# Scan stage of a hybrid block on one core: the drives of two states by TensorE from diagonal matrices, one state left to GpSimd, ScalarE's five placed anew

## What is computed

```python
def selective_scan(u, dt, A, Bm, Cm, Dvec):
    dA  = exp(dt[..., None] * A)                        # decay of state n
    dBu = dt[..., None] * Bm[:, :, None, :] * u[..., None]   # drive of state n
    def step(h, xs):
        dA_t, dBu_t, C_t = xs
        h = dA_t * h + dBu_t
        return h, einsum('bdn,bn->bd', h, C_t)
    ys = scan(step, 0, over the tokens)
    return ys + u * Dvec
```

## Time and profile before

| | |
|---|---|
| median of 3 runs | 2160.12 us (2157.04 to 2160.7) |
| profiled execution, its own time | 2158.89 us |
| its span, first to last instruction | 2157.1 us |
| scan stage | from about 780 to 1592 us of the span |
| busy over the span | PE 93%, PEld 71%, DVE 69%, ACT 56%, POOL 67% |
| mean granted TensorE clock | 0.977 |

### The profile page before, as it was taken

The page is one execution under the profiler, slowest core; times in us unless marked ns, Lnnn a source line. Parts: engine busy times, 40 slices in busy tenths (PEclk is TensorE's granted clock), DMA queues, the critical chain, the costliest instruction groups (busy, mean ns, idle before and its releaser), DMA issues. The chain is left out here.

```text
span 2157.1 us, 42455 instructions
## 1 busy us (share of the span) xinstructions
PE 2008.0 (93%) x14350; PEld 1535.7 (71%) x14351; DVE 1497.0 (69%) x2749; ACT 1201.5 (56%) x2399; POOL 1440.7 (67%) x972
## 2 busy tenths in 40 slices
PE   7998999999999988989988889898789999999998
PEld 5886448999999545656655556565554489999994
DVE  6887684333333579999999999999976833333335
ACT  5775423222222279999989888989844132222222
POOL 6774005777767249999999999989940067777670
PEclk9999999999999989999999999989899999999999
DMA  8000100000001422332322323222233000000014
GB/s 304 0 1 11 30 1 20 26 24 25 24 24 26 111 96 90 101 106 93 100 89 100 99 89 98 100 91 97 83 138 143 1 22 26 24 26 24 24 25 121
DMA packets 72198, 141.91 MB, mean 66 GB/s; under 512 B 9835, under 2 KB 43629, under 8 KB 69910
## 3 DMA queue, kind: packets, MB, share of 16 engines
q1 hardware_dynamic: 62998, 121.86, 16.9%
q0 software_dynamic: 9088, 18.63, 3.0%
HBM read 123.81 MB, written 16.65 MB: 65 GB/s over the span
## 5 line engine op out<-in xcount | busy, mean ns | idle before, releaser
L2269 POOL TENSOR_TENSOR m_seen<-m_state,experts 128x1024 f32<-128x1024 f32 x256 | 600.7, 2369 | 59.8 <-DVE m_state L2323 54.2
L2323 DVE TENSOR_TENSOR_SCAN m_state<-experts,ps 128x512 f32<-128x512 f32 x448 | 540.1, 1235 | 0.5 <-PE ps L1860 0.5
L1877 PE MATMUL ps<-ident,m_seen 128*128 128x128 f32 x2048 | 278.8, 281 | 36.9 <-POOL m_seen L2269 36.9
L1877 PEld LDWEIGHTS ps<-ident,m_seen 128*128 128x128 f32 x2048 | 243.2, 145 | 75.8 <-POOL m_seen L2269 54.9
L2082 ACT ACTIVATE experts<-delta,experts 128x512 f32<-128x512 f32 x448 | 291.3, 713 | 1.0 <-DVE delta L2349 0.5
L1591 POOL COPY f_weights<-experts 128x1898 f32 x142 | 252.3, 1777 | 23.8 <-issue 23.5
L1414 PE MATMUL first_up_ps<-f_xT,f_weights 128*128 128x128 f32 x1988 | 241.4, 275 | 1.7 <-issue 1.7
L1414 PE MATMUL ps<-zu,f_weights 128*128 128x128 f32 x1988 | 241.4, 275 | 1.7 <-issue 1.7
L1414 PEld LDWEIGHTS first_up_ps<-f_xT,f_weights 128*128 128x128 f32 x1988 | 233.2, 192 | 2.5 <-issue 2.5
L1414 PEld LDWEIGHTS ps<-zu,f_weights 128*128 128x128 f32 x1988 | 233.2, 192 | 2.5 <-issue 2.5
L2303 DVE TENSOR_TENSOR ps<-m_delta_u,ps 128x512 f32<-128x512 f32 x286 | 193.4, 676 | 15.4 <-PE ps L1835 15.1
(11 more groups left out here) (451 smaller groups left out, 3904.2 us busy)
## 6 DMA issues: line engine op xcount, KB each, us to landing
experts<-m_rows SPq DMA_DIRECT2D x144, 512.0 KB, 3.6
experts<-in_experts SPq DMA_DIRECT2D x17, 1461.0 KB, 18.6
tokens<-f_rows SPq DMA_DIRECT2D x8, 512.0 KB, 5.3
f_rows<-expert_out SPq DMA_DIRECT2D x8, 512.0 KB, 7.0
f_cols<-expert_out SPq DMA_DIRECT2D x8, 512.0 KB, 7.0
out<-X SPq DMA_DIRECT2D x4, 512.0 KB, 3.2
X<-in_x SPq DMA_DIRECT2D x4, 448.0 KB, 5.9
f_xin<-tokens,f_take POOLq DMA_INDIRECT x71
```

The source lines that it names most:

```text
L1877: mm = pe.matmul(Y[:, i // 2, at:at + P], seen[:, n % SEEN, h, i * P:(i + 1) * P], ident[:], is_transpose=True, start=(n == 0 and at == 0) ...
L2269: pool.tensor_tensor(seen[:, n % SEEN], state[:, n % RING], c_rep[:, Q % C_RING, n % C_GROUP, :].unsqueeze(1).to_broadcast([P, HALF, SEG]) ...
L2323: dve.tensor_tensor_scan(state[:, n % RING, h, :], decay_, drive_, before_, ALU.mult, ALU.add).then_inc(s_state, 1)
```

## The change

- AWAY is state 12 alone; GpSimd makes its drive after step 4 (before: state 4 after step 15 of the unit before, state 12 after step 6).
- DIAGONAL = (2, 11): the drive of these two comes from TensorE alone. `cross` multiplies, for each of the four pieces i of 128 tokens, the turned delta_u (tokens on the partitions, 128 by 128) with a diagonal matrix whose diagonal holds B's row for these tokens; the result is the drive, channels on the partitions, in PSUM. Four fp32 multiplications of 128 by 128 a half.
- The diagonal matrices (128 by 4 * 128 for each of the two states) are laid out by DMA: a DRAM array m_diagonal is written once with zeros from an SBUF tile that GpSimd has cleared (512 KB); in each unit SP scatters the 512 numbers of a row onto the diagonals (elements of 4 bytes, L1776 of the changed kernel) and loads the matrix (256 KB, L1785) ahead of the second and the third group of C.
- ACROSS = (4, 6, 8, 10, 14): ScalarE still scales for five states, but others, at steps 0, 3, 5, 6 and 10 (before: state 2 at step 15 of the unit before, 5 at 1, 8 at 3, 11 at 6, 14 at 9).
- VectorE multiplies the drives of 8 states (0, 1, 3, 5, 7, 9, 13, 15) for 9 (0, 1, 3, 6, 7, 9, 10, 13, 15).
- The decay of state 4 goes into the ring dA like the others, at step 1; those of 5 and 6 are made at steps 2 and 3.
- b_rep holds one row for two.

```diff
-                AWAY = (4, 12)
-                AWAY_AT = {15: 4, 6: 12}
-                ACROSS = (2, 5, 8, 11, 14)
-                ACROSS_AT = {15: 2, 1: 5, 3: 8, 6: 11, 9: 14}
+                AWAY, AWAY_AT = 12, 4
+                ACROSS = (4, 6, 8, 10, 14)
+                ACROSS_AT = {0: 4, 3: 6, 5: 8, 6: 10, 10: 14}
+                DIAGONAL = (2, 11)
+                WIDTH = len(DIAGONAL) * SEG
...
+                DIAGONAL_BEFORE = (1, 2)
...
+                diagonal = lodge(WIDTH).rearrange("p (k t) -> p k t", t=SEG)
+                diagonal_out = nc.dram_tensor("m_diagonal", (P * (WIDTH + 1),), F32, kind="Internal").ap()
+                whole_out = diagonal_out[0:P * WIDTH].rearrange("(p k t) -> p k t", k=len(DIAGONAL), t=SEG)
+                entries_out = diagonal_out.rearrange("(p f) -> p f", f=WIDTH + 1)[:, 0:WIDTH:P].rearrange("p (k i) -> p k i", i=SEG // P)
...
-                DECAYED = [[2, 3], [5], [6], [4], [], [7, 8], [9], [10], [11], [], [13], [12], [14], [15], [NS], [NS + 1]]
+                DECAYED = [[2, 3], [4], [5], [6], [], [7, 8], [9], [10], [11], [], [13], [12], [14], [15], [NS], [NS + 1]]
...
+                        sp.wait_ge(s_hT, 1)
+                        sp.dma_start(whole_out, diagonal).then_inc(s_rows_out, 16)
+                        sp.wait_ge(s_rows_out, 16)
...
-                            sp.wait_ge(s_rows_out, 16 * (V + 1))
-                            wait(sp, s_away, len(AWAY) * V)
-                            sp.dma_start(b_rep, rows_out[V % 2][AWAY[0]:NS:AWAY[1] - AWAY[0], :].unsqueeze(0).to_broadcast([P, len(AWAY), SEG])).then_inc(s_b_rep, 16)
+                            sp.wait_ge(s_rows_out, stored(V))
+                            for k, n in enumerate(DIAGONAL):
+                                wait(sp, s_diagonal[k], 16 * V)
+                                sp.dma_start(entries_out[:, k, :], rows_out[V % 2][n, :].rearrange("(i p) -> p i", p=P), allow_slow_non_contiguous=True).then_inc(s_rows_out, 16)
+                            wait(sp, s_away, V)
+                            sp.dma_start(b_rep, rows_out[V % 2][AWAY:AWAY + 1, :].to_broadcast([P, SEG])).then_inc(s_b_rep, 16)
                             for g in range(GROUPS):
+                                if g in DIAGONAL_BEFORE:
+                                    k = DIAGONAL_BEFORE.index(g)
+                                    sp.wait_ge(s_rows_out, stored(V) + 16 * len(DIAGONAL))
+                                    if V:
+                                        sp.wait_ge(s_upright, (nth_upright[(V - 1) * NS + DIAGONAL[k]] + 1) * HALF)
+                                    sp.dma_start(diagonal[:, k, :], whole_out[:, k, :]).then_inc(s_diagonal[k], 16)
...
+                        def cross(G, h):
+                            U, n = divmod(G, NS)
+                            k = DIAGONAL.index(n)
+                            pe.wait_ge(s_diagonal[k], 16 * (U + 1))
+                            pe.wait_ge(s_read0, nth0["du", U] + 1)
+                            pe.wait_ge(s_read1, nth1["du", U] + 1)
+                            wait(pe, s_state, (G - B_RING) * HALF + h + 1)
+                            for i in range(TILES):
+                                mm = pe.matmul(PB[n % B_RING][:, h, i * P:(i + 1) * P], across[:, i, h * P:(h + 1) * P], diagonal[:, k, i * P:(i + 1) * P], start=True, stop=True)
+                            mm.then_inc(s_upright, 1)
...
                         def refill(G, h):
+                            if G % NS in DIAGONAL:
+                                cross(G, h)
...
-                        scale(ACROSS[0])
...
-                            if n + 1 == AWAY[0]:
-                                decays(G + 1)
...
+                        pool.memset(diagonal, 0.0)
                         pool.memset(hT[:, :, 0:PAD], 0.0).then_inc(s_hT, 1)
...
-                        drive(AWAY[0])
                         for G in range(STEPS):
...
-                            if n in AWAY_AT:
-                                m = AWAY_AT[n] + (NS if AWAY_AT[n] < n else 0)
-                                if U * NS + m < STEPS:
-                                    drive(U * NS + m)
+                            if n == AWAY_AT:
+                                drive(U * NS + AWAY)
```

More of the change, by code:

```diff
@@ L1658, in mamba @@
                 scaled = lodge(SCALED * TILES * DI).rearrange("p (r i d) -> p r i d", r=SCALED, d=DI)
+                diagonal = lodge(WIDTH).rearrange("p (k t) -> p k t", t=SEG)
+                assert room[0] <= LODGERS * EXPERT
+                diagonal_out = nc.dram_tensor("m_diagonal", (P * (WIDTH + 1),), F32, kind="Internal").ap()
+                whole_out = diagonal_out[0:P * WIDTH].rearrange("(p k t) -> p k t", k=len(DIAGONAL), t=SEG)
+                entries_out = diagonal_out.rearrange("(p f) -> p f", f=WIDTH + 1)[:, 0:WIDTH:P].rearrange("p (k i) -> p k i", i=SEG // P)
                 rows_out = [nc.dram_tensor(f"m_rows_{k}", (2 * NS, SEG), F32, kind="Internal").ap() for k in range(2)]
@@ L1682, in mamba @@
                 s_turned, s_back, s_y = ts("turned"), ts("back"), ts("y")
+                s_diagonal = [ts(f"diagonal{k}") for k in range(len(DIAGONAL))]
                 s_scaled, s_upright, s_hT = ts("scaled"), ts("upright"), ts("hT")
@@ L1699, in tokens, with stored @@
                     return (t // C * STREAMS + s) * TPB + t % C * TILES
+                def stored(V):
+                    return 16 * (2 + V * (1 + len(DIAGONAL)))
                 def columns_in(U, k):
@@ L1732, in mamba @@
                 decayed = [0, 1] + [U * NS + m for U in range(N_UNITS) for n in range(NS) for m in DECAYED[n] if U * NS + m < STEPS]
-                assert all(n + 1 not in AWAY or DECAYED[n][-1] == n + 1 for n in range(NS))
+                assert DECAYED[AWAY - 1][-1] == AWAY
                 nth_decay = {G: k for k, G in enumerate(decayed)}
-                driven = [G for G in range(STEPS) if G % NS not in AWAY + ACROSS]
+                driven = [G for G in range(STEPS) if G % NS != AWAY and G % NS not in ACROSS + DIAGONAL]
+                nth_upright = {G: k for k, G in enumerate(G for G in range(STEPS) if G % NS in ACROSS + DIAGONAL)}
+                turned_over = [G for G in range(STEPS) if G % NS in ACROSS]
                 nth_across = {G: k for k, G in enumerate(G for G in range(STEPS) if G % NS in ACROSS)}
                 nth_drive = {G: k for k, G in enumerate(driven)}
-                nth_away = {G: k for k, G in enumerate(G for G in range(STEPS) if G % NS in AWAY)}
                 kept = [(U, n) for U in range(N_UNITS) if UNITS[U][2] % C < C - 1 for n in range(0, NS, 2)]
@@ L2041, in round_high @@
                             act.wait_ge(s_rows, V + 1)
-                            wait(act, s_rows_out, 16 * V)
+                            if V:
+                                act.wait_ge(s_rows_out, stored(V - 1))
                             act.activation(bc[0:XR], SIDE1[0:XR], ACT.Copy).then_inc(s_bc, 1)
-                            wait(act, s_b, (V - 1) * (NS - len(AWAY) - len(ACROSS)) * HALF)
+                            wait(act, s_b, (V - 1) * (NS - 1 - len(ACROSS) - len(DIAGONAL)) * HALF)
                             act.activation(parts[0:32, V % 2, :], SIDE1[0:32], ACT.Copy).then_inc(s_rounded, 1)
@@ L2075, in decays @@
                                 act.wait_ge(s_dt, U + 1)
-                            if n not in AWAY:
+                            if n != AWAY:
                                 wait(act, s_state, (G - DECAYS + 1) * HALF)
                             for h in range(HALF):
-                                if n in AWAY:
+                                if n == AWAY:
                                     act.wait_ge(s_state, (G - B_RING) * HALF + h + 1)
                                 lhn = (l * HALF + h) * NS + n
-                                act.activation(PB[n % B_RING][:, h, :] if n in AWAY else dA[:, n % DECAYS, h, :], delta[:, U % 2, h, :], ACT.Exp, scale=decay[:, lhn:lhn + 1]).then_inc(s_decay, 1)
+                                act.activation(PB[n % B_RING][:, h, :] if n == AWAY else dA[:, n % DECAYS, h, :], delta[:, U % 2, h, :], ACT.Exp, scale=decay[:, lhn:lhn + 1]).then_inc(s_decay, 1)
                         def columns_b(V):
@@ L2099, in scale @@
                             act.wait_ge(s_read1, nth1["du", U] + 1)
-                            wait(act, s_upright, (k - SCALED + 1) * HALF)
+                            if k >= SCALED:
+                                act.wait_ge(s_upright, (nth_upright[turned_over[k - SCALED]] + 1) * HALF)
                             for i in range(TILES):
@@ L2184, in _ @@
                             for m in DECAYED[n]:
-                                if m != AWAY[0] and (m < NS or V < N_UNITS):
+                                if m < NS or V < N_UNITS:
                                     decays(U * NS + m)
```

16 lines of the change are left out of this document (9 added, 7 removed).

## The result

The changed kernel takes **2174.28 us** (median of 4 runs, 2173.99 to 2176.27) against 2160.41 before: ratio 1.0064, 95% interval 1.0052 to 1.0076, so slower by 13.9 us. The forecast was 2168 and slower, range 2147 to 2181: the sign and the range held. Of the loss it had 9 us, put on top of the profiled execution of before (2158.9), or 7.6 over the median, where 13.9 came. The execution profiled took 2176.27 us (span 2174.4).

A forecast was written before the change was run, and what follows sets the result against it. ScalarE and VectorE were taken to bind together at the quick pace, VectorE alone at the slow. Pairs +8.5, three plain units +2, first 0, last -1.2: together +9 on the profiled 2158.9, so 2168 us; range 2147 to 2181.

The forecast's parts named there:

- ScalarE's chain: ScalarE's work up to scan 12, then VectorE to scan 9's end; E to X forecast from 54.3 to 56.8 us.
- the first rival: VectorE's relief shows: products' time gained, -9.4 us (2149.5) with GpSimd's hold, -18.7 (2140) without; chance 0.18.
- I take 0.45 for four: TensorE's price in us for four fp32 multiplications with a diagonal, taken from a row of sixteen at 1.79.
- E to D keeps 17.8: GpSimd's order from scan 9 on is unchanged, so this stretch stays 17.8 us.
- the two-unit sum: Plain period as half of E to X, X to D and D to E: 49.45 us against 48.5, quick pace.
- the four points E, D, Y and X: E: scan 9's end; D: second drive of next unit's state 0; Y: ScalarE's copy of the sum; X: scan 12's start.
- the ring of one unit: Found afterwards, not forecast: ScalarE to softplus end, GpSimd through state 14's product, TensorE to next sum copy; 51.4 us.
- Plain units at the start: First three units after the first, without VectorE's extra add: forecast +2 us together.
- Six pairs at +8.5, the last unit at -1.2, the first at 0: Later units paired plain plus add unit (VectorE adds 1.5 us); the last has no next unit for ScalarE.
- dear multiplication: Rival: four diagonal products on TensorE take 0.88 us, +7 more, 2175; chance 0.05.
- The waits: VectorE waiting for ScalarE before scan 12: 2 to 4 us in most plain units, 20 to 35 in all.
- Clock: Rival: longer waits idle TensorE and its clock drops, 1.2 us per such unit; ten more give 2180; chance 0.12.

The follow-up runs named there:

- experiment 3: Changed kernel with all four taps of the convolution's second half at step 2, ahead of state 4's upright: 2159.89 us, 14.4 less than the changed kernel.
- experiment 4: Changed kernel with ScalarE's scaling for state 8 left out (drive not the reference's): 2160.56 us, 13.7 less than the changed kernel.
- experiment 10: Kernel before with VectorE's two products for state 10 cut to 8 columns, nothing put on another engine: 2158.29 us against 2160.12.
- Experiment 9: Changed kernel with each product with a diagonal replaced by a transposition of the same block: 2168.93 us.
- experiment 8: Changed kernel with the scatters and loads of the two diagonals made in the first unit only: 2174.53 us.
- Experiment 2: Changed kernel with ScalarE's copy of the kept states put ahead of the scaling in each step: 2174.71 us.
- experiment 6: Version of the change: diagonal for state 11 alone, GpSimd driving 4 and 12, ScalarE scaling 2, 5, 8, 10, 14: 2160.02 us against 2161.76 before.
- experiment 11: Changed kernel with all taps at step 2, state 6's scaling at step 1, decays of 7 and 8 ahead of the convolution's copy: 2157.59 us.
- experiment 7: Changed kernel with each product with a diagonal made twice into the same place: 2225.43 us, 51 more than the changed kernel.

## Why the forecast was right, and where it fell short

- *Slower, by ScalarE's chain: right.* The order of work between Y and X grew and the relief did not pay. Forecast 33 us from Y to X, measured 32.5 to 34.1. Experiments 3 and 4 show that taking 1.6 to 1.8 from there ends the loss; experiment 10 shows that VectorE's relief is worth 1.8 us by its median and 4.3 at the far end of its interval, against the 9.4 to 18.7 of the first rival. The path was another than the forecast had: it closed ScalarE's chain over X and VectorE, and it closes over the end of the softplus and GpSimd.
- *"I take 0.45 for four": wrong, and the costliest one.* I read x16 in the earlier trace rows as sixteen multiplications; they were eight with two records each, so the row says 0.22 for one, and four take 0.89. The convolution's wait was 2.00 to 2.3 (once 2.77), not 1.6 to 1.8. The Trainium skill, FP8 and Floating Point Precision (TensorE Precision Notes), gave 0.85 by estimate, and the trace agrees within 5%; the forecast had set it aside for a row that was misread. Experiment 9 puts this step at about 5 us. The rival with 0.05 for it, "2175", is the time that came.
- *"E to D keeps 17.8", the two-unit sum: wrong in form.* GpSimd's order from scan 9 on was indeed unchanged, but its second piece, delta, waits for ScalarE's softplus, which the four points E, D, Y and X leave out. GpSimd never waited there before; now it did, 5.4 us in 11 of 15 units, and Y follows GpSimd. The sum halves a delay, (56.8 + 12.0 + 30.1)/2, that in the ring of one unit is paid whole once its 1 us of air is used up. Plain units at the start were put at +0.7 to +0.95 each and lost 2.5: 7.6 us where the forecast had 2.
- *Six pairs at +8.5, the last unit at -1.2, the first at 0: too much in all.* The pairs and the last unit together were put at +7.3 and measured +3.7 (+6.8 and -3.1); the first Y, by experiment 8 (841.25 for 839.73), came 1.5 later. Before, the later units lasted 50.5 on the mean already, held through GpSimd by VectorE; the ring had to rise from 48 to their length before anything was lost, which is why they lost less each than the first three. So the plain units and the product were put too low and the pairs too high: that the sum came as near as it did is partly luck, and that the "dear multiplication" rival's 2175 fits, too.
- *The waits: too low and in the wrong place.* They came to 46 us, 9.6 of it before scan 12, where the forecast had 20 to 35. Experiment 2 moved the wait of scan 8 to scan 10 and the time stayed. The pairs last 101.0 to 102.8, where 100.4 to 101.7 was given as the sign of being right.
- *DMA at nothing: right.* The scatter landed in 3.1 us, and experiment 8 has no gain without it. *Clock: no part in the loss.* It was granted at 0.981 over the span, before 0.977, and at 0.96 in the scan stage of both. In experiment 3's scan stage it was 0.99, so a part of what that run gave back over the stage may be the clock's; this was not separated. In the unit shown it was 0.97 in both, and the 1.75 us are those of ScalarE's wait.

What stays open: the floor of 2157 to 2160 at which experiments 3, 4, 6, 10 and 11 all come to rest. In the traces of 3, 4 and 11 nine of fourteen units lead back over GpSimd to VectorE's scan 9, so these two with TensorE's last stretch are the likely hold; no run took work from GpSimd alone to try it. No run either took away the scaling of state 14, which should be worth nothing if the ring closes over GpSimd and would be worth up to 1.6 a unit if it closed over X. Nor is it known why scans run at two paces.

## What to carry to other kernels

Find the loop whose pieces follow each other without air (that they add up to the period proves nothing), and ask of each moved operation whether it lies in it; the fullest engine gains nothing from relief while such a loop is as long as its own work. For each engine with little air, look up how long before its start every input was ready: an input that came 1 us early and is now to come 3 us later is the next hold, though the old trace shows no wait for it. Before a row is used as a price, count its records against the calls in the program.

## What was not expected of the hardware

- An fp32 multiplication of 128 by 128 leaves two records and takes 0.22 us, a transposition of the same block one record and 0.11 (4 in 0.89 and 0.44).
- A scatter of 512 single elements lands in 3.1 us, as fast as a 64 KB store (3.2 in the earlier trace rows), and leaving out thirty of the thirty-two changed nothing here (experiment 8).
- TensorE, at 44 of 50 us busy before, had no slack in the places that matter: of 57 us added in experiment 7, 51 were paid.
